# The second half's cap, gain and weighting moved in the first stage, and unread products of ones in TensorE's pauses there and in the banded head

## What is computed

```python
x = x + attn_i(cond_i(x, side, side, w, u, time))     # i = 0..3: linear, banded, grouped, selective
x = x + ffn_i(cond2_i(x, side, side, w, u, time))     # top-1 experts, LoRA experts, int8, top-4 experts
```

```python
ek, ekv = exp(min(k, 30)), exp(min(k, 30)) * v        # k = v = side
nf, df = scan(a * decay + ekv), scan(b * decay + ek)   # forwards; nb, db backwards
euk = exp(min(u + k, 30))
num, den = nf + nb - ekv + euk * v, df + db - ek + euk
out = sigmoid(x) * num / max(den, 1e-8) * (0.8 + 0.2 * tf)
```

## Time and profile before

| | |
|---|---|
| median of 3 timed runs | 1679.03 us |
| profiled execution, own time | 1684.12 us |
| its span, first to last instruction | 1682.9 us |
| mean granted TensorE clock | 0.953 |
| TensorE products busy | 1505.1 us (89%) |
| VectorE busy | 1212.1 us (72%) |
| ScalarE busy | 895.7 us (53%) |
| GpSimd busy | 355.5 us (21%) |

### The profile page before, as it was taken

One profiled execution on the slowest core, in us unless ns is written; L12 is line 12 of the kernel. 1 busy time (PEld: TensorE's weight loads), 2 busy tenths in 40 slices (PEclk: granted clock), 3 DMA queues, 4 the chain that ended last, 5 costly groups with the idle time before them and its releaser, 6 DMA issues. The chain is left out here.

```text
span 1682.9 us, 16508 instructions
## 1 busy us (share of the span) xinstructions
PE 1505.1 (89%) x5247; PEld 822.8 (49%) x5258; DVE 1212.1 (72%) x1972; ACT 895.7 (53%) x1611; POOL 355.5 (21%) x228
## 2 busy tenths in 40 slices
PE   4998899799899999977999999766888888899998
PEld 1565465378544444433555555322333333467776
DVE  8586587456466367488898988576999999746665
ACT  5444377445323213367788888457856534234443
POOL 1000432231001001000000000000288877023332
PEclk8999999889899999988999999887999999999999
DMA  4001594270300000022121212102000000111110
GB/s 132 1 1 38 213 325 156 70 121 1 152 0 0 0 16 1 29 60 76 26 74 24 78 26 64 48 21 82 0 1 0 1 1 0 42 43 53 54 43 26
DMA packets 45852, 88.23 MB, mean 52 GB/s; under 512 B 10082, under 2 KB 27444, under 8 KB 43462
## 3 DMA queue, kind: packets, MB, share of 16 engines
q1 hardware_dynamic: 40678, 61.48, 12.7%
q0 software_dynamic: 5088, 25.69, 4.3%
HBM read 70.49 MB, written 7.22 MB: 46 GB/s over the span
## 5 line engine op out<-in xcount | busy, mean ns | idle before, releaser
L3003 POOL TENSOR_TENSOR s_bu<-s_rep,s_du 128x1024 f32<-128x1024 f32 x64 | 150.6, 2356 | 551.8 <-ACT s_rep L2871 516.1
L2818 DVE TENSOR_TENSOR_SCAN s_bu<-bank,s_bu 128x1024 f32<-128x1024 f32 x64 | 146.0, 2282 | 3.7 <-POOL s_bu L3003 2.0
L159 PE MATMUL bank<-e_xs,e_wsp 128*128 128x512 f32 x528 | 127.8, 391 | 0.7 <-issue 0.7
L3108 PE MATMUL bank<-s_bu,ident 128*128 128x512 f32 x256 | 122.7, 602 | 0.7 <-DVE s_dl L2775 0.2
L2887 ACT ACTIVATE bank<-s_dl,s_an 128x510 f32<-128x510 f32 x128 | 82.8, 684 | 53.2 <-DVE s_bu L2818 53.2
L159 PEld LDWEIGHTS bank<-e_xs,e_wsp 128*128 128x128 f32 x528 | 99.0, 188 | 22.8 <-issue 1.9
L159 PE MATMUL bank<-r_am,r_b 128*128 128x512 f32 x240 | 106.0, 592 | 1.4 <-DVE r_am L1754 1.4
L1812 ACT ACTIVATE r_sl<-bank 128x512 f32<-128x512 f32 x28 | 16.7, 597 | 133.1 <-PE bank L159 133.0
L3218 DVE TENSOR_TENSOR e_s<-e_s,bank 128x512 f32<-128x512 f32 (+1 forms) x50 | 34.4, 688 | 69.7 <-ACT e_s L3350 69.7
L159 PE MATMUL bank<-conditioned,g_wqk 128*128 128x512 f32 x160 | 79.3, 621 | 4.1 <-ACT g_th L2254 3.8
L3350 ACT ACTIVATE e_s<-bank 128x512 f32<-128x512 f32 (+1 forms) x50 | 30.0, 599 | 97.1 <-PE bank L159 97.1
(11 more groups left out here) (518 smaller groups left out, 3556.5 us busy)
## 6 DMA issues: line engine op xcount, KB each, us to landing
g_turn<-g_q SPq DMA_DIRECT2D x64, 128.0 KB, 2.3
e_wgu<-in_e_gu SPq DMA_DIRECT2D x22, 256.0 KB, 2.6
b_vw<-b_values SPq DMA_DIRECT2D x48, 64.0 KB, 3.4
e_wd<-in_e_down SPq DMA_DIRECT2D x22, 128.0 KB, 2.6
r_w<-in_r_w SPq DMA_DIRECT2D x3, 896.0 KB, 7.8
g_wqk<-in_g_qk SPq DMA_DIRECT2D x4, 640.0 KB, 3.9
g_wgv<-in_g_gv SPq DMA_DIRECT2D x4, 640.0 KB, 4.1
g_wo<-in_g_wo SPq DMA_DIRECT2D x4, 512.0 KB, 3.7
```

What stands on the lines that cost most here:

```text
L159: last = e.matmul(out, lhs, rhs, start=start and n == 0, stop=stop and n == len(pairs) - 1, skip_group_check=True)
L2818: e.tensor_tensor_scan(b, flat(k.pairs[n % 2][:, :, :]), b, 0.0, ALU.mult, ALU.add).then_inc(k["s_scanned"].up(), 1)
L3003: e.tensor_tensor(m.bu[n % m.NBU][:, :, :], m.rep[:, 2 * np:2 * np + 2, :], m.du[:, et, half(h)].unsqueeze(1).to_broadcast([P, 2, HALF]), ...
L3108: summed = e.matmul(banks[6][:, :], k.ident[:, :], m.bu[(n - 1) % m.NBU][:, i, :], start=np == 0 and i == 0, stop=np == m.NP - 1 and i == ...
```

## The change

The second half's cap (`start_capped`) moves from between the first scans to behind the first half's terms, and its exponents stand between the two factors. Its gain and its weighting move into `linear_vector`: the gain behind the reduction of the weights, the weighting behind the scans of the second half. ScalarE's exponential of the second half and its `first_exp` move behind `first_inverse` of the first half. The sum for a numerator is split: its first two addends wait only for the scans, the third for the product. TensorE sums the squares ahead of `l_partq`, and makes queries and keys ahead of both denominators of the second half; VectorE normalises before it scans the second half. The new `keep_busy` issues products of `ones` with `ones` into a bank that nobody reads before it is written again: 3 and 4 in the first stage, 4, 2 and 4 in the banded head.

```diff
--- before.py
+++ after.py
@@ -369,6 +369,7 @@
     h, ct = q // 2, q % 2
     if h:
         e.wait_ge(*k["first_den"].at(q - 1))
+        e.wait_ge(*k["first_terms"].at(5 * q - 5))
     e.tensor_scalar(k.euk[:, half(ct)], k.kv[:, ct, half(h)], k.vcol("cond_u", ct), 30.0, ALU.add, ALU.min).then_inc(k["first_exponent"].up(), 1)
 
 
@@ -449,16 +450,16 @@
     start_gain(k, e, 0)
     e.wait_ge(*k["first_zero"].at(2))
     first_back(k, e, 0)
-    start_capped(k, e, 1)
     first_back(k, e, 1)
     start_weighted(k, e, 0)
     first_terms(k, e, 0)
     first_cap(k, e, 0)
     first_cap(k, e, 1)
     first_terms(k, e, 1)
-    start_gain(k, e, 1)
+    start_capped(k, e, 1)
     first_factor(k, e, 0)
-    start_weighted(k, e, 1)
+    first_exponent(k, e, 2)
+    first_exponent(k, e, 3)
     first_factor(k, e, 1)
     first_condition(k, e, 0)
 
@@ -496,12 +497,14 @@
     start_exp(k, e, 0)
     first_exp(k, e, 0)
     first_exp(k, e, 1)
-    start_exp(k, e, 1)
     linear_decays(k, e)
     e.wait_ge(*k["load_x"].at(16))
     for h in range(NH):
         e.activation(k.XC[:, :, half(h)], k.XT[:, :, half(h)], ACT.Sigmoid).then_inc(k["sigmoid"].up(), 1)
     first_inverse(k, e, 0)
+    start_exp(k, e, 1)
+    first_exp(k, e, 2)
+    first_exp(k, e, 3)
 
 
 def first_den_tensor(k, e, q):
@@ -515,10 +518,12 @@
 
 def first_num_tensor(k, e, q):
     ct = q % 2
-    e.wait_ge(*k["first_terms"].at(5 * q + 5))
+    e.wait_ge(*k["first_terms"].at(5 * q + 4))
     if q >= 2:
         e.wait_ge(*k["first_ready"].at(q - 1))
-    mm(e, k.banks[4 + ct][:, :], [(k.ident[:, :], a[:, half(ct)]) for a in (k.nf, k.nb[0], k.db[0])]).then_inc(k["first_num"].up(), 1)
+    mm(e, k.banks[4 + ct][:, :], [(k.ident[:, :], a[:, half(ct)]) for a in (k.nf, k.nb[0])], stop=False)
+    e.wait_ge(*k["first_terms"].at(5 * q + 5))
+    mm(e, k.banks[4 + ct][:, :], [(k.ident[:, :], k.db[0][:, half(ct)])], start=False).then_inc(k["first_num"].up(), 1)
 
 
 
@@ -603,12 +608,12 @@
     m, banks = k.linear, k.banks
     by_head = m.heads[:, :].unsqueeze(2).to_broadcast([P, 8, 16])
     ternary_mean(k, e, m.wqkv, m.partq, "load_l0_qkv")
-    first_exponent(k, e, 2)
-    first_exponent(k, e, 3)
+    start_gain(k, e, 1)
     ternary_round(k, e, m.wqkv, m.partq, 768 * C, 0, banks[7][:, 0:1])
+    norm_apply(k, e, 0, 0, k.XC, m.rs, "l0_qkv_norm", m.sq)
     first_back(k, e, 2)
-    norm_apply(k, e, 0, 0, k.XC, m.rs, "l0_qkv_norm", m.sq)
     first_back(k, e, 3)
+    start_weighted(k, e, 1)
     first_cap(k, e, 2)
     e.wait_ge(*k["load_l0_decay"].at(64))
     e.wait_ge(*k["l0_lambdas"].at(3))
@@ -744,8 +749,6 @@
     m, banks = k.linear, k.banks
     norm_square(k, e, k.XC, m.sq, 0, (k["conditioned"], 1))
     norm_root(k, e, 0, 0, m.rs, 2.0 ** -23, banks[0])
-    first_exp(k, e, 2)
-    first_exp(k, e, 3)
     linear_query_scalar(k, e, 0)
     linear_key_scalar(k, e, 0)
     e.wait_ge(*k["l0_zeroed"].at(4))
@@ -808,6 +811,13 @@
     mm(e, k.banks[0][:, :], [(m.wqkv[:, c, C + t * P:C + (t + 1) * P], m.sq[:, c, half(h)]) for c in range(CT)]).then_inc(k["l0_k"].up(), 1)
 
 
+def keep_busy(k, e, bank, n):
+
+    ones = k.ones[:, :].unsqueeze(1).to_broadcast([P, 4, P])
+    for _ in range(n):
+        e.matmul(bank[:, :].rearrange("p (a t) -> p a t", a=4), k.ones[:, :], ones, start=True, stop=True, skip_group_check=True)
+
+
 def linear_tensor(k, e):
     m, banks = k.linear, k.banks
     e.wait_ge(*k["constants"].at(7))
@@ -816,15 +826,17 @@
     first_den_tensor(k, e, 1)
     first_num_tensor(k, e, 0)
     first_num_tensor(k, e, 1)
+    keep_busy(k, e, banks[6], 3)
+    e.wait_ge(*k["squares"].at(1))
+    mm(e, banks[0][:, :], [(k.ones[:, :], m.sq[:, c, half(0)]) for c in range(CT)]).then_inc(k["square_sums"].up(), 1)
     e.wait_ge(*k["ternary_part"].at(1))
     mm(e, banks[7][:, 0:1], [(k.ones[:, :], m.partq[:, 0:1])]).then_inc(k["ternary_sum"].up(), 1)
-    e.wait_ge(*k["squares"].at(1))
-    mm(e, banks[0][:, :], [(k.ones[:, :], m.sq[:, c, half(0)]) for c in range(CT)]).then_inc(k["square_sums"].up(), 1)
+    keep_busy(k, e, banks[6], 4)
     e.wait_ge(*k["ternary_ready"].at(1))
+    linear_query_tensor(k, e, 0)
+    linear_key_tensor(k, e, 0)
     first_den_tensor(k, e, 2)
-    linear_query_tensor(k, e, 0)
     first_den_tensor(k, e, 3)
-    linear_key_tensor(k, e, 0)
     linear_values_tensor(k, e, 0)
     first_num_tensor(k, e, 2)
     first_num_tensor(k, e, 3)
@@ -1545,14 +1557,17 @@
 
 def banded_tensor(k, e):
     m, banks = k.banded, k.banks
+    keep_busy(k, e, banks[3], 4)
     for h in range(NH):
         conditioned(k, e, 2, h)
         mm(e, banks[h][:, :], [(k.ones[:, :], k.XC[:, c, half(h)]) for c in range(CT)]).then_inc(k["b_sum"].up(), 1)
+    keep_busy(k, e, banks[3], 2)
     norm_tensor(k, e, 2, m.squares())
     e.wait_ge(*k["load_b"].at(96))
     mm(e, banks[2][0:m.NG, 0:C], [(m.gl[:, c, :], m.wv[:, c, :]) for c in range(CT)]).then_inc(k["b_vg"].up(), 1)
     for i in range(2):
         mm(e, banks[3][:, tile(i, m.NG)], [(m.wk[:, c, tile(i)], m.gl[:, c, :]) for c in range(CT)]).then_inc(k["b_kg"].up(), 1)
+    keep_busy(k, e, banks[0], 4)
     e.wait_ge(*k["b_biased"].at(1))
 
     def project(h, hh, w, bank, done):
```

## The result

| | before | changed |
|---|---|---|
| median of the timed runs | 1675.72 us (6 runs) | 1664.24 us (6 runs) |
| ratio, 95% interval | | 0.9932 [0.9908, 0.9955] |
| the same kernel again | 1674.93 us (35 runs) | 1666.47 us (12 runs), 0.9945 [0.9923, 0.9967] |
| profiled execution, span | 1682.9 us | 1666.7 us |
| mean granted clock | 0.953 | 0.966 |

Faster by 9 to 11 us, where 6.4 were forecast. The median of 1664.24 us lies inside the range of 1663 to 1680, and outside the forecast's own range of 1669 to 1677. The forecast counted from 1679.03, the median of the kernel before in three runs; in six runs that median is 1675.72, so 3.3 of the 8.4 us between the forecast of 1672.6 and the 1664.24 measured are the starting point. A gain of more than 0.5% had been given 0.32, a change within 0.5% had 0.62: the less likely one came.

The account below looks back on a forecast made before the run. Waits on the first stage's path and half-clock spells behind TensorE pauses were taken as the price. Head 2.0 or 4.0 plus third stage 2.5 or 4.4, one gain failing: 6.4 us, 1679.03 to 1672.6; range 1669 to 1677, all cases 1663 to 1680.

Parts of the forecast that it names:

- The steps of the first stage: Predicted first-stage times: conditioned half 26.4, rounding 31.0, normalising ended 35.85, terms 46.2, second half's first numerator 48.6 us.
- The fall in the pause of 2.7 us: First stage, uncovered TensorE pause before the second half's first numerator: clock falls, costing 2.0 us; held likelier at 0.65.
- Pauses up to 2.00 held: Argument for neither uncertain gain failing: TensorE pauses up to 2.00 us had left the clock up in the trace.
- The order's own: First stage: the reordering itself brings the conditioned half forward from 28.69 to 26.4 us, 2.3 us.
- rival 3: Unread products in first and third stages meet the lower clock and outlast their pauses: 8.0 us slower, 1687; chance 0.06.
- the head's 4.0: First stage: its unit loop starts 4.0 us earlier, at 55.2, if the clock doesn't fall.
- the 59.24: Start in us of the first stage's 16-unit loop in the kernel before; the first half's worth is what this moves.
- GpSimd first, gain 0: Third stage: GpSimd's residual sum starts before VectorE's centring, which waits, so the earlier means gain 0; held likelier at 0.55.
- 315.98: Third stage: start in us of GpSimd's residual sum, taken to lead VectorE's centring, ready at 316.05, by 0.07 us.
- The sum: Whole kernel: head 2.0 or 4.0 plus third stage 2.5 or 4.4, with exactly one uncertain gain failing: 6.4 us.
- the case of 2.0 and 4.4: Head gains 2.0 us because the clock falls; third stage gains 4.4 because VectorE goes first.
- rival 2: Neither uncertain gain fails, in first-stage clock or third-stage turn: 8.4 us faster, 1670.6; chance 0.20.

Follow-up runs that it names:

- the order alone: The changed kernel without any of its 17 unread products, so only the reordering and split numerator, against the kernel before: 1675.35 us, 1.0012 [0.9987, 1.0037].
- the banded head alone: The kernel before plus only the 10 unread products of the third stage's banded head: 1670.96 us, 0.9977 of the kernel before.
- filled pause: The changed kernel plus three unread products before the second half's first numerator in the first stage: 1665.53 us, 0.9939 of the kernel before.
- changed again: The changed kernel profiled and timed a second time without any edit: ratio 0.9945 to the kernel before.
- block loop's product: The changed kernel plus one unread product in the third stage's block loop, before the first transposes: 1664.63 us, 0.9934 of the kernel before.
- all three edits: The changed kernel plus three unread first-stage products, GpSimd's residual sums waiting for VectorE's centrings, and one unread block-loop product: 1663.42 us, 0.9919 of the kernel before.
- changed first stage alone: The changed first stage with its seven unread products, banded head as in the kernel before: 1670.1 us, 0.9976 of the kernel before.

## Why the prediction was right, and where it wasn't

- **The steps of the first stage** came out within 0.2 us in the first profile: conditioned half 26.43 (26.4), rounding 30.93 (31.0), normalising ended at 35.7 (35.85), terms 46.28 (46.2), first numerator 48.76 (48.6). In the other profiles of this order the conditioned half comes at 26.5 to 27.2.
- **The fall in the pause of 2.7 us** (0.65): it came in four of the five profiles that have this pause behind a warm head of the stage, for 3.4 or 6.8 us, not in the fifth, nor in the order alone, and not in the two where the pause is filled. It costs 1.2 to 2.7 us, where 1.3 to 2.6 were put down. The loop start of 56.65 is inside 55.2 to 57.8; the 6.8 us of low clock (58.12) are more than the 5.2 I allowed.
- **"Pauses up to 2.00 held"** was read too far. In the kernel before, the clock was up at 150.97 behind that pause, but fell at about 153.7, 1.6 us after that product had ended, and three profiles have 13.7 us of low clock shortly after the pause of 1.54 us in the block loop, the profile that the forecast read among them. So these traces show no length of pause that is safe.
- **"The order's own" gain, about 2.3 us,** failed, in rival 3 and in the way the head's 4.0 was built up. The order alone gains nothing (60.44, 1.0012), and the unread products on the old order gain all that the new order has with its pauses filled (loop start 55.47 and 55.45), 0.9966 in the whole. I followed the new order with the full clock and never the old one with it. The five profiles whose first stage is the old one start the loop at 57.52 to 59.37, so the clock is worth 2.0 to 3.9 us there; the 59.24 from which the forecast counted is near the late end. At the full clock the new order has the half conditioned 2.0 us earlier (26.58 with the pause filled, 28.62 in the old order) and the normalising started 3.5 us earlier (34.46, 37.92), but the second half's numerator terms start 0.6 us later (46.43, 45.86), because the second half's denominators stand behind the keys.
- **GpSimd first, gain 0** (0.55) failed as the likelier. Of the five profiles with a warm banded head and no added wait, GpSimd was first in one (the banded head alone), VectorE in two (changed, filled pause), and in two VectorE did not wait at all, because GpSimd, its cast held up by the first centring, began 0.05 us after the second had begun (changed again, block loop's product). From the start of the sums to the first projections it takes 19.4 us in the first case, 17.5 in the second and 15.7 in the third, 19.4 before: gains of 0 and 1.9, both as forecast, and a third one of 3.7 that the forecast didn't have. I had taken 315.98 as fixed; it hangs on a mask's load and on that cast, and came 2.4 to 4.3 us after the sums' start. The exclusive turn itself is shown, by a wait that removes the meeting: centrings of 1.23 and 1.22 us on the kernel before, 1.30 and 1.22 with all three edits. So is the Trainium skill's rule of an exclusive lock (SBUF — State Buffer, SBUF: two separate sides) borne out: over the profiles a centring that meets a residual sum lasts 1.36 to 3.38 us, by the moment at which it comes, and always ends 1.1 us after that sum.
- **The sum** of 6.4 is under the 9 to 11 measured, though inside the second interval (5.5 to 12.9 us). In the first profile the clock fell, as held likelier, and VectorE was first, as held less likely: 2.6 and 4.5 us, together 7.1, near the case of 2.0 and 4.4 that the sum took. By the timed runs the head gives 4.0 and the third stage 3.9; their sum, 7.9, is rival 2 but for 0.5 us, but intervals this wide don't choose between the forecast and rival 2. The rest, up to 3 us, the intervals don't separate from nothing; a share may be the spell in the block loop, absent in both profiles of the changed kernel and present in both of the kernel before, but that it is caused by the change is not shown: with warm banded head alone it was there, with the cold head of the order alone it was not. That the median fell inside the range owes much to the 4 us put on either side.

## What to carry to other kernels

Before reordering around a stall, price the old order at the full clock as well as the new one: here products nobody reads, in two pauses of the old order, brought the loop as far forward as the reorder with three pauses filled. Such products have to end before the real work is ready; here they did in every profile. And look for a GpSimd instruction beside a VectorE one with two inputs on the path: one wait that puts it later took 3.6 us out of the place and gave 0.9966 [0.9945, 0.9987]. Not run here: the old order with its two pauses filled, the warm banded head and that wait together, the simplest kernel that these experiments suggest.

## What the runs showed of the hardware

- A pause of 2.68 us was followed by a fall of the clock in the same kernel's two executions, once for 3.4 and once for 6.8 us; in two other kernels with this pause (order alone, changed first stage alone) no fall followed. One of 1.54 us in the block loop was followed by 13.7 us of low clock in three of the eleven profiles whose block loop is unedited, and by nothing in eight. Between the first pair of profiles that spell cost 4.9 us, with the same instructions in the loop.
- In the block loop TensorE is busy 13.48 of 13.70 us and the clock stays low, mostly with short products (128x64, 128x128); it is back to 1.00 at 372.2, behind a group of 128x512 products that starts at 368.65. What ended the spell was not tested.
- A VectorE instruction with two inputs and a GpSimd one waited until the other had ended: the centrings end 1.1 us after GpSimd's sum in every profile where they are blocked, and GpSimd's cast took 1.28 to 1.36 us instead of 0.29 in the three where it met a centring.
- The timed runs of the kernel before lie between 1669 and 1686 us, and the longer ones have the lower granted clock: in the last comparison 12 of 29 are at 1679 or more, at 0.954 in the mean, the others at 0.960. With GpSimd behind the centrings none of 12 lay over 1672, with all three edits on the changed kernel none of 9 over 1665.
